# The last two periods of a software-pipelined kernel written out in another order

## The reference

```python
Af = A_grid[None] * f[:, None]
Bf = B_grid[None] * f[:, None]
gradv_Af = _grad(Af[:, 0], 1) + _grad(Af[:, 1], 2)
gradvv_Bf = _grad2(Bf[:, 0], 1) + _grad2(Bf[:, 1], 2) + _grad(_grad(Bf[:, 2], 2), 1) + _grad(_grad(Bf[:, 2], 1), 2)
df = -gradv_Af + gradvv_Bf * 0.5
f_new = f + df * dt[:, None, None]
return jnp.maximum(f_new, 0.0)
```

## Time and profile before

| | us |
|---|---|
| median of 3 runs | 895.62 |
| lowest and highest | 894.95, 899.71 |
| the profiled execution | 897.77 |
| its span, first to last instruction | 896.0 |
| TensorE busy (matmul) | 817.8 |
| VectorE busy | 739.6 |
| ScalarE busy | 623.2 |
| GpSimd busy | 163.8 |

### The profile page before, as it was taken

The page is one execution under the profiler, slowest core; times in us unless marked ns, Lnnn a source line. Parts: engine busy times, 40 slices in busy tenths (PEclk is TensorE's granted clock), DMA queues, the critical chain, the costliest instruction groups (busy, mean ns, idle before and its releaser), DMA issues.

```text
span 896.0 us, 18592 instructions
## 1 busy us (share of the span) xinstructions
PE 817.8 (91%) x5968; PEld 698.8 (78%) x5968; DVE 739.6 (83%) x2474; ACT 623.2 (70%) x1284; POOL 163.8 (18%) x160
## 2 busy tenths in 40 slices
PE   5576869899999999999999999999999999998692
PEld 2355658788988888888888888888888888787581
DVE  5452787898998989898989899898989898969555
ACT  3153758687878787887878787878788787777230
POOL 3010101222030302122222213030212212201200
PEclk9677989999999999999999999999999999999986
DMA  6356978577585868676676857595758678581110
GB/s 173 117 129 159 206 173 195 129 173 178 133 192 149 190 153 173 156 187 164 157 185 168 189 134 179 151 193 154 183 156 177 162 155 175 138 200 43 53 36 12
DMA packets 147593, 137.33 MB, mean 153 GB/s; under 512 B 19282, under 2 KB 144787, under 8 KB 147492
## 3 DMA queue, kind: packets, MB, share of 16 engines
q1 hardware_dynamic: 147172, 135.80, 63.8%
q10 hardware_dynamic: 320, 0.26, 0.1%
HBM read 98.23 MB, written 4.23 MB: 114 GB/s over the span
## 4 chain that ended last, share of the span: by engine, by line
PE 82%; DVE 9%; issue 3%; SPq 2%; DMA 2%; ACT 1%; POOL 0%; POOLq 0%; DVEq 0%; ACTq 0%
PE back_bank L1109 12%; PE turn_bank L1065 11%; PE score_bank L1184 6%; PE context_bank L1119 6%; PE score_bank L1185 6%; PE front_bank L1103 5%; PE back_bank L1103 5%; PE attend_bank L1103 5%; PE front_bank L1136 3%; PE back_bank L1089 3%; PE front_bank L1290 3%; PE back_bank L1080 3%; PE attend_bank L1089 3%; PE attend_bank L1050 2%; PE front_bank L1338 2%
## 5 line engine op out<-in xcount | busy, mean ns | idle before, releaser
L548 ACT ACTIVATE sc<-sc,negmax 128x256 f32<-128x256 f32 x512 | 231.2, 504 | 20.6 <-DVE negmax L905 20.1
L905 DVE CUSTOM_DVE_ANT_0 sc<-score_bank,side 128x256 f32<-128x256 f32 x512 | 195.3, 419 | 40.4 <-PE score_bank L1185 33.0
L526 ACT ACTIVATE pt<-turn_bank 128x512 f32<-128x512 f32 x176 | 105.9, 602 | 133.3 <-PE turn_bank L1065 112.3
L1065 PE MATMUL turn_bank<-ident,sc 128*128 128x128 f32 x1024 | 158.4, 278 | 1.4 <-ACT sc L548 1.4
L1065 PEld LDWEIGHTS turn_bank<-ident,sc 128*128 128x128 f32 x1024 | 124.3, 142 | 32.6 <-issue 14.1
L1184 PE MATMUL score_bank<-ks,qs 128*128 128x256 f32 x512 | 124.0, 324 | 8.5 <-DVE negmax L905 6.2
L1109 PE MATMUL back_bank<-w,ffT 128*128 128x256 f32 x512 | 118.0, 379 | 0.0
L1109 PEld LDWEIGHTS back_bank<-w,ffT 128*128 128x128 f32 x512 | 97.0, 190 | 12.6
L1185 PE MATMUL score_bank<-mask_neg,ident_r 128*128 128x512 f32 x256 | 102.8, 402 | 0.0
L468 POOL TENSOR_TENSOR rstd<-var,half_neg 128x2 f32<-128x2 f32 x64 | 50.0, 781 | 286.9 <-DVE var L830 285.3
L1184 PEld LDWEIGHTS score_bank<-ks,qs 128*128 128x128 f32 x512 | 79.6, 195 | 16.6 <-issue 7.9
(11 more groups left out here) (216 smaller groups left out, 1978.1 us busy)
## 6 DMA issues: line engine op xcount, KB each, us to landing
side<-in_side SPq DMA_DIRECT2D x128, 512.0 KB, 5.4
qs<-qh SPq DMA_DIRECT2D x128, 64.0 KB, 4.3
qs<-ql SPq DMA_DIRECT2D x128, 64.0 KB, 4.6
wb<-in_wb SPq DMA_DIRECT2D x16, 512.0 KB, 7.2
ks<-kh SPq DMA_DIRECT2D x126, 64.0 KB, 4.1
ks<-kl SPq DMA_DIRECT2D x126, 64.0 KB, 4.5
xN<-in_x SPq DMA_DIRECT2D x16, 256.0 KB, 4.8
wc<-in_wc SPq DMA_DIRECT2D x16, 256.0 KB, 3.1
```

The source lines that it names most:

```text
L526: e.activation(pt[:, h % NP2, :, :], two(tbank[h % 2]), ACT.Copy).then_inc(copied[h % 4], 1)
L548: i = e.activation(sc[:, h % NS, q, :], sc[:, h % NS, q, :], ACT.Exp, bias=negmax[:, q, h:h + 1], scale=-1.0)
L905: i = e.tensor_tensor_reduce(sc[:, s % NS, q, :], two(sbank[s % 2])[:, q, :], side[:, (H * X.i + s) % NSIDE, q, :], -1.0, 3.4e38, ALU.add, ...
L1065: i = e.transpose(tbank[h % 2][:, k * S + q * P:k * S + q * P + P], sc[:, h % NS, q, k * P:k * P + P], ident[:, :])
```

## The change

For periods 16 and 17 (and 18, folded into 17) `body` returns at once on TensorE, VectorE and ScalarE, and `last_turns` writes their instructions out in an order of its own. The stages are now helper functions that both call, with the same operations in them. For t below 16 every engine has the same instructions in the same order as before. On GpSimd, in period 16, the power for sample 15's n3 comes ahead of the one for sample 14's x4. The first layer of sample 15 goes to the banks abank, bbank, abank, fbank in turn instead of bbank, abank, bbank, abank. The L2 weights of sample 15 are loaded into the tile of the scores, `sc`, once the last head is turned, instead of into `wb`.

```diff
+        wb_last = sc[:, 0:A2 // P // TT, :, :].rearrange("p a t x -> p (a t) x")
...
+        LAST_BANKS = (abank, bbank, abank, fbank)
...
+                    if is_step(t, s, NB, 2):
+                        kind = e.value_load(ids_ok[0:1, 2, bass.ds(B.i, 1)], min_val=0, max_val=NC2 - 1)
+                        head(e, turned, B, H - 1)
+                        e.dma_start(wb_last, d["wb"][bass.ds(kind, 2)].rearrange("c (k p) n -> p (c k) n", p=P)).then_inc(ld_late, 16)
+                    if s == 0 and T and T.i < NB - 1:
                         kind = e.value_load(ids_ok[0:1, 2, bass.ds(T.i, 1)], min_val=0, max_val=NC2 - 1)
...
-                    if s == 7 and T:
+                    if s == 7 and T and t != NB:
                         power(T, 3, ev["x4_var"], ev["x4_rstd"])
                     if s == 8 and B:
                         power(B, 2, ev["x2_var"], ev["x2_rstd"])
+                    if is_step(t, s, NB, 8):
...
+            def last_turns():
+                G, F, X, B, T, U = phases(NB)
+                kind = e.value_load(ids_ok[0:1, 2, bass.ds(T.i, 1)], min_val=0, max_val=NC2 - 1)
+                exponentials(B, H - 1)
+                copy_turned(B, H - 2)
+                copy_turned(B, H - 1)
+                copy_context_hi(B)
+                copy_context(B)
+                copy_x3(T)
+                relu_out(U)
+                condition(T, kind)
+                high_n3(B)
+                for j, bank in enumerate(LAST_BANKS):
+                    first_ff(B, j, bank)
+                    tanh_ff(B, j)
+                high_r2(T)
+                high_u(T)
+                G, F, X, B, T, U = phases(NB + 1)
+                kind = e.value_load(ids_ok[0:1, 2, bass.ds(T.i, 1)], min_val=0, max_val=NC2 - 1)
+                copy_x3(T)
+                condition(T, kind)
+                relu_out(U)
+                high_r2(T)
+                high_u(T)
+                relu_out(T)
             def body(t):
+                if t == NB:
+                    last_turns()
+                if t >= NB:
+                    return
...
+            def last_turns():
+                G, F, X, B, T, U = phases(NB)
+                low_u(U)
+                first_context(B)
+                second_context(B)
+                sum_x3(T)
+                sum_w(U)
+                step_w(U)
+                sum_x2(B)
+                norm_apply(B, 2, n3, x2, ev["x2_rstd"], ev["n3_ready"])
+                low_n3(B)
+                sum_x4(T)
+                gate_ff(B, 0)
+                scale_x4(T)
+                gate_ff(B, 1)
+                shift_x4(T)
+                gate_ff(B, 2)
+                product_r2(T)
+                inner_u(T)
+                gate_ff(B, 3)
+                product_r1(T)
+                sum_u(T)
+                low_r2(T)
+                G, F, X, B, T, U = phases(NB + 1)
+                low_u(U)
+                sum_x3(T)
+                for x in (U, T):
+                    if x is T:
+                        sum_x4(T)
+                        scale_x4(T)
+                        shift_x4(T)
+                        product_r2(T)
+                        inner_u(T)
+                        product_r1(T)
+                        sum_u(T)
+                        low_r2(T)
+                        low_u(T)
+                    grid_product(x, t_a, grid_a, "ga_ready")
+                    grid_product(x, t_b, grid_b, "gb2_ready")
+                    grid_product(x, t_c, grid_c, "gc_ready")
+                    inner_e(x)
+                    sum_e(x)
+                    sum_w(x)
+                    step_w(x)
...
+            def differ_when_ready(x):
+                for m, parts, ready in ((d2T, (r2_h, r2_l), "r2l_ready"), (d1T, (u_h, u_l), "ul_ready")):
+                    e.wait_ge(ev[ready], x.n)
+                    for q in range(TT):
+                        for k in range(KT):
+                            for n, part in enumerate(parts):
+                                i = e.matmul(two(fbank)[:, q, :], m[:, k, q * P:q * P + P], part[:, k, :], start=(m is d2T and q == 0 and k == 0 and n == 0),
+                                             stop=(m is d1T and q == TT - 1 and k == KT - 1 and n == 1))
+                i.then_inc(ev["d_done"], 1)
...
+            def last_turns():
+                G, F, X, B, T, U = phases(NB)
+                kind = e.value_load(ids_ok[0:1, 2, bass.ds(T.i, 1)], min_val=0, max_val=NC2 - 1)
+                quarter(e, "ff_ready", T, 2)
+                second_ff(T, ((1, 0), (1, 1), (1, 2), (1, 3), (0, 4), (0, 5)), no_more)
+                four(flips(B, H - 2))
+                four(flips(B, H - 1))
+                quarter(e, "ff_ready", T, 3)
+                second_ff(T, ((0, 6), (0, 7), (1, 4)), no_more)
+                mix(B, 3)
+                e.wait_ge(ev["ct_lo"], B.n)
+                gather(B, 0, ev["c1_lo"])
+                second_ff(T, ((1, 5), (1, 6), (1, 7)), no_more).then_inc(ev["w2_done"], 1)
+                e.wait_ge(ev["ct_hi"], B.n)
+                e.wait_ge(ev["ctxn_lo"], B.n)
+                gather(B, 1, ev["c1_hi"])
+                e.wait_ge(ev["r2l_ready"], U.n)
+                e.wait_ge(ev["ul_ready"], U.n)
+                differ(U, 0)
+                e.wait_ge(ev["ctxn_hi"], B.n)
+                turn(abank, ctxN, ev["c2_turned"])
+                differ(U, 1)
+                e.wait_ge(ev["ctxT_ready"], B.n)
+                project(abank, ctxT, wo, ev["wo_done"], no_more)
+                e.wait_ge(ev["x3_ready"], T.n)
+                turn(bbank, x3, ev["x3_turned"])
+                e.wait_ge(ev["x3T_ready"], T.n)
+                e.wait_ge(ld_kind, times(T, 32))
+                condition(T, kind, wb)
+                e.wait_ge(ev["n3_ready"], B.n)
+                turn(abank, n3, ev["n3_turned"])
+                e.wait_ge(ev["gb_ready"], T.n)
+                project(bbank, gbT, wc, ev["c_done"], no_more)
+                e.wait_ge(ev["n3l_ready"], B.n)
+                for j, bank in enumerate(LAST_BANKS):
+                    if j == 1:
+                        e.wait_ge(ev["x4_ready"], T.n)
+                    if j == 2:
+                        quarter(e, "u1_ready", B, 0)
+                    if j == 3:
+                        e.wait_ge(ev["w_ready"], U.n)
+                    project_T_parts(bank, w1, w1l, 2 * P * j, n3h, n3l, 2, ev["w1_done"])
+                quarter(e, "u1_ready", B, 1)
+                quarter(e, "ff_ready", B, 1)
+                second_ff(B, ((0, 0), (0, 1), (0, 2), (0, 3)), no_more)
+                G, F, X, B, T, U = phases(NB + 1)
+                kind = e.value_load(ids_ok[0:1, 2, bass.ds(T.i, 1)], min_val=0, max_val=NC2 - 1)
+                quarter(e, "ff_ready", T, 2)
+                second_ff(T, ((1, 0), (1, 1), (1, 2), (1, 3), (0, 4), (0, 5)), no_more)
+                quarter(e, "ff_ready", T, 3)
+                second_ff(T, ((0, 6), (0, 7), (1, 4), (1, 5), (1, 6), (1, 7)), no_more).then_inc(ev["w2_done"], 1)
+                e.wait_ge(ev["r2l_ready"], U.n)
+                e.wait_ge(ev["ul_ready"], U.n)
+                differ(U, 0)
+                e.wait_ge(ev["x3_ready"], T.n)
+                turn(bbank, x3, ev["x3_turned"])
+                differ(U, 1)
+                e.wait_ge(ev["x3T_ready"], T.n)
+                e.wait_ge(ld_kind, times(T, 32) - 16)
+                e.wait_ge(ld_late, 7 * 16)
+                condition(T, kind, wb_last)
+                e.wait_ge(ev["gb_ready"], T.n)
+                project(bbank, gbT, wc, ev["c_done"], no_more)
+                e.wait_ge(ev["w_ready"], U.n)
+                differ_when_ready(T)
```

293 lines of the change are left out of this document (180 added, 113 removed).

## The result

| | before | changed |
|---|---|---|
| median, us | 895.29 of 4 runs | 887.04 of 4 runs |
| lowest and highest | 894.2, 899.71 | 886.78, 887.92 |
| the profiled execution, its span | 897.77, 896.0 | 887.92, 886.1 |

The ratio is 0.990 with an interval of 0.9866 to 0.9934, 8.3 us. The forecast was 883.9, 11.7 us under the median of 895.62 that was known then; 887.04 lies outside the forecast's own range of 881.5 to 886 and inside the wider one, 880.8 to 888. One execution of the kernel before, in the comparison of e1 to e4, took 2085.14 us and is left out of the ratios and medians.

What follows compares the result with a forecast made beforehand. TensorE was the bound until the last two periods, there two chains of engines waiting on each other. Gains 8.0 + 0 + 3.7 = 11.7 us off the 895.62 median gave 883.9, own range 881.5 to 886, wider 880.8 to 888.

Steps and rivals of the forecast that it cites:

- Period 16 up to the first layer: Reordered start of period 16: sample 15's first layer would start at 845.1 instead of 851.32, a gain of 6.2 us.
- the turn of x3 and the condition of sample 14, 0.44 and 1.73 with a copy between them, done before: TensorE work placed in the gap between x2 and n3 of sample 15, letting n3 be turned at 842.95.
- First layer to the end of the second: Sample 15's two layers in period 16: second layer ends at 858.8 instead of 866.8, 1.8 us gained in this part.
- Full clock: TensorE's clock would stay full through sample 15's two layers, which then take 4 x 1.42 + 6.91 = 12.6 us.
- GpSimd's hold: GpSimd's add of b2 for sample 15 would slow VectorE's gates, costing 1.1 us, bounds 0 and 1.4.
- To x4: From sample 15's second layer to its x4: same order as before, 7.67 us, so 0 us gained.
- The block on VectorE: Sample 14's products and sums, moved ahead of sample 15's x4, would end at 865.5, before x4's date of 866.4.
- The end: Sample 15's last stage: low parts first, matmuls beside VectorE's e part, last add at 887.5 not 891.25, 3.75 us gained.
- list of signs: Dates expected in the new profile, among them the Relu about 13.7 + 1.5 us behind sample 15's x4.
- rival 2: TensorE's clock falls in period 16 all the same, costing 3 to 6 us: 887 to 890, chance 0.14.
- (3): Sample 14's x4 on VectorE holds up sample 15, costing 3 to 5 us: 887 to 889, chance 0.09.
- (4): No gain or slower: the new load on SyncE's queue makes things late, more than 900.1 us, chance 0.02.

Runs made afterwards that it cites:

- e1: The changed kernel measured again with no edit: ratio 0.9873 to the kernel before, medians 897.29 and 885.87 us.
- e4: Kernel before plus 15 unread TensorE matmuls ahead of sample 15's turn of n3: ratio 0.9974; last score matmul to end 71.89 us, against 71.98.
- e7: Changed kernel with TensorE's waits for x3T and weights moved inside its branch: last score matmul to end 59.82 us, against 60.94.
- e10: Changed kernel with period 16's first half mostly in the old order, attention pieces late: last score matmul to end 65.69 us, against 60.94.
- e5: Kernel before plus unread TensorE matmuls, 15 ahead of the turn of n3 and 8 behind: ratio 0.997; last score matmul to end 69.12 us, against 71.98.
- e6: Changed kernel with GpSimd's add of b2 for sample 15 moved ahead of the gates: last score matmul to end 59.98 us, against 60.94.
- e9: Changed kernel with the first layer's fourth quarter back in its old bank, plus waits: last score matmul to end 61.17 us, against 60.94.
- e2: Kernel before with only sample 15's last stage in the new order: ratio 0.9956; last score matmul to end 68.43 us, against 71.98.
- e3: Changed kernel with sample 15's last stage as before: 0.9917 of the kernel before; last score matmul to end 64.51 us, against 60.94 for changed.
- e8: Changed kernel plus 34 unread TensorE matmuls ahead of sample 15's last derivatives: last score matmul to end 60.91 us, against 60.94.

## Why the prediction came out as it did

Where the date of the changed trace is used, 1.20 us are taken off.

**Period 16 up to the first layer**, 6.2 forecast, 5.6 measured in the chain (the table goes by the first record, which lies 0.35 ahead of the end of the matmuls before it, and so has 5.94 here and 1.76 in the next part). The context was turned at the date forecast, x2 came at 839.14 (forecast 838.9) and n3 was turned at 842.7 (843.93 less 1.20; forecast 842.95). That n3 was early behind a late x2 is a gain the forecast hasn't: 3.59 us instead of 4.01, since VectorE's n3 took 0.73 instead of 1.02 and GpSimd's power 0.72 instead of 0.85. In the kernel before each ran beside an instruction of the other engine that the new order has moved away; no run undoes this alone. The error in this part is in "the turn of x3 and the condition of sample 14, 0.44 and 1.73 with a copy between them, done before": between the copy and the condition lie 0.66 us of TensorE's branch, which in the kernel before lay beside a gather in this period. So the Gelu was late for the second product, and that for the first layer. e7 takes the 0.66 away and gives 0.55 back. Of the 5.55 us at x2, e10 shows 4.58 to be the order of the attention pieces; the rest, the output projection ahead of L2's second product, is read from the traces and not tested alone.

**First layer to the end of the second**, 1.8 forecast, 2.1 measured by the chain (15.45 to 13.34). Full clock as forecast; that the clock is worth 2.4 us there is shown by e5. GpSimd's hold was taken as 1.1 us and cost VectorE 1.04, but TensorE only 0.73 (e6), since its first four matmuls kept it busy until 854.36 in any case. The Trainium skill's "GPSIMD Engine Reference", section Specifications, names instructions with two SBUF inputs among those that contend with GpSimd: fN is one, and the trace agrees (1.92 against 0.88).

**To x4**, 0 forecast, 0.2 lost (7.89 against 7.67 us). u's low part of sample 14 was ready only at 860.17, so that sample 14's derivatives started at 860.32, 0.05 behind the end of the second layer; in the kernel before they start 0.36 ahead of that end. Where it is ready in time (e6, e9, e10) the 0.22 us are gone. The block on VectorE ended at 867.15 by its last multiply-add, 1.0 ahead of x4; that cover held, GpSimd's second hold (grid_c, 1.79 instead of 0.69) in it. The weights in `sc` were never waited for.

**The end**, 3.75 forecast, 3.56 measured (e2, e3). VectorE comes last, by 0.47 us instead of 0.3, and the clock is worth nothing (e8): right as put. (The prediction's list of signs has the Relu 13.7 + 1.5 us behind x4, its own working 13.06 + 1.5; it came 14.76 behind.) The last add is 13.25 us behind x4 and not 13.06 (887.5 - 874.44), for waits of VectorE on its own and ScalarE's results that in the old order lay behind other work.

**Sum**: 11.7 forecast, 11.04 measured in the traces (71.98 - 60.94) and 11.4 in e1's comparison. The mechanism was right in its main parts, with small errors of both signs. The 883.9 was 3.1 us below the median it was held against: 0.7 for the links above, and the other 2.4 are put down to the heads of those executions, most of which have no trace; the forecast took the head as fixed. So 887.04 fell outside the forecast's own range, and that the wider range held it is luck: its upper end of 888 was there for rivals 2 and 3, and neither came true.

**The rivals**: the clock did not fall in period 16 (2), x4 of sample 14 held nobody (3; TensorE's second quarter followed the first without a gap), and the new load was hidden (4). That rival 2 was real, e4 and e10 show: there the clock fell although no wait ahead of the fall was longer than 1.08 us.

## What to carry to other kernels

When a pipeline drains, its slots' order is a leftover of the full pipeline: write the longest remaining chain first and put the other sample's work into its waits, and look at the list of the engine that ends last for work that could also be done later, because no other engine needs it yet. Then look for what the old order hid: here a branch taken after a wait instead of during it (0.5 to 0.6 us a time) and an add on GpSimd that slid onto VectorE's critical instructions (1.04 us on VectorE, 0.73 on the chain). Where the head of a program wanders by several us, compare traces from a fixed instruction on; dates then agree to 0.1 us and effects of a few tenths can be read from one execution each, as long as the granted clock is the same in both: look at it first.

## What the runs showed that was not expected

- The same instructions took between 818.0 and 829.6 us up to one fixed matmul. VectorE's first score instruction of period 3 starts between 200.0 and 211.7 us, and from it to the anchor it is 617.8 to 618.7 us in all fourteen traces: all but 0.9 us of the spread arises ahead of it. That the medians differ for the same reason is likely and not shown, since most executions have no trace.
- 0.66 us pass on TensorE from the arrival of an operand to the first matmul when a branch lies between; 0.05 and 0.13 us when the branch was taken before.
- Around the turn of n3, waits of 0.82 and 1.83 us went with a fall of the granted clock to 0.50 (e4, 0.96 us into the second), waits of 1.20 and 1.41 in the same place did not (e10). Yet in e10 it had fallen a little earlier, behind waits of 1.08 and 0.69. The length of the waits alone doesn't tell whether it falls; what does, these runs leave open.
